# A decoder on one core: causal state products become masked score matrices, and three other stages are reordered

## The chip, the cores and the metric

The kernel runs on one core of a Trainium2 chip. A core has TensorE (matrix products, written to PSUM), VectorE, ScalarE, GpSimd and SyncE (which here only issues transfers). The metric is the device time of one execution in microseconds.

## The reference, cut to what matters

The whole kernel is a decoder of twelve layers on x of 32 x 128 x 128 (items, positions, features). The change touches the layers below. The second self attention (`_L1_attn_ref`) is a linear attention that learns at test time, with 16 heads of 8 features. Per head it takes two gradient steps and applies the states up to each position. In the form that the kernel uses, with k, q and v projected from the normalised x, W0 the first weights of a head, and tril the causal sum over positions s <= t:

```python
z1 = k @ W0
dz1 = gradient(z1, v)                         # of a layer norm of z1 against v, per head
z2 = z1 - sum_{s<=t} (k[t] . k[s]) * dz1[s]
dz2 = gradient(z2, v) + dz1
out = q @ W0 - sum_{s<=t} (q[t] . k[s]) * dz2[s]
x = x + group_norm(out) @ Wout + bout
```

The sum over s can be made in two ways: as a running state (an 8x8 matrix for each head and position, summed along the positions, then multiplied by k or q), or as a 128x128 matrix of products k[t].k[s] for each head, masked, times dz.

The other layers: `_L1_ffn_ref`, 64 experts with six chosen per token and a shared one of 176 hidden features, whose sum is added to x; `_L2_attn_ref`, a linear attention without heads, relu(q), relu(k), out = q @ (k^T v) / (q . sum k); and `_L3_xattn_ref`, a cross attention with 16 heads of 8 features on 120 context rows with softmax.

## The kernel before

x stays in SBUF for the whole kernel, `R.x`, 128 positions x 32 items x 128 features. Each layer is a phase: its own buffers and semaphores, one program for each engine, and a barrier of all engines at its end. Within a phase each engine's program is an order written out by hand. `skewed(eng, depth, n)` yields slots; in slot t, `item(lag)` stands for item t - lag, so that an engine's slot holds steps of up to depth + 1 items, each at another point of its way. The body is unrolled four times in a hardware loop, with the first and last slots outside. `written_out` does the same with no loop. `chain(...)` makes the next instruction of the same engine wait for this one. All matrix products here are f32, except biases; TensorE runs each as two instructions, each with its own load of the stationary matrix.

`l1_attn` works on pairs of items (sixteen slots with work, depth 3). ScalarE normalises, TensorE transposes and projects to five groups of 128 columns (q, k, v scaled by the norm's weights, k @ W0, q @ W0). VectorE computes `gradient` (ten operations on 256 columns), then the outer products of k and dz, 1,024 columns per item (L1203, L1214); TensorE sums them along the positions by a product with the triangular `upper` (L1260, two of 512 columns per item); VectorE multiplies the sums out of PSUM by k or q (L1158) and reduces eight columns to one (L1161). All of this is done twice per pair, for step 1 and step 2. GpSimd prepares x + bout (L1104).

`l1_slots` runs the experts on 32 pairs of experts' slots, two at a time: transfer of 128 rows and the weights, transpose (L1848), hidden products (L1855), Silu and product, output (L1863), a scatter to DRAM by GpSimd. `l1_combine` reads the six shares of each token back, reduces them on VectorE (L1908), adds the shared expert (L378, L381, L387) and makes statistics. `l2_attn` starts with a common power on GpSimd (L95) and then goes through pairs of items, two at a time.

`l3_xattn` (depth 4) per item: scores (L2921), maxima on VectorE (L2858), their transpose (L2946), scores again in the other orientation (L2950), minus the maxima by products with `pick` (L2961), exponential on ScalarE (L2909), values (L2935). The first scores of the next item use the same PSUM as the exponential, so they wait for it. Other layers that the rows show: `l_mix_p_conv` (L2393, a convolution in `l2_mix`, 128x128 stationary and 32 moving columns) and L634 (`l0_xattn`).

## Time and profile before

| | us |
|---|---|
| median of 3 runs | 4386.25 |
| lowest and highest | 4383.8, 4393.79 |
| the profiled execution, its time | 4399.44 |
| its span, from first to last instruction | 4397.5 |
| TensorE, VectorE, ScalarE, GpSimd busy | 3267.4, 2842.7, 1802.4, 681.8 |
| `l1_attn`, stretch 827 to 1364 | 537.0 |
| `l1_slots`, 1764 to 1856 | 92.0 |
| `l1_combine`, 1856 to 1953.4 | 97.4 |
| `l2_attn`, 1953.4 to 2079.4 | 126.0 |
| `l3_xattn`, 3696 to 3993 | 297.0 |

PE is TensorE, PEld its loads of stationary matrices, DVE VectorE, ACT ScalarE, POOL GpSimd, SPq SyncE's queue. Names have buffer numbers left out, so `l_attn` may be the self attention of any layer; the line tells which. PEclk, the granted clock of TensorE, is a share of 2.4 GHz: 1.00 is that, 0.50 is 1.2 GHz. A busy TensorE is not TensorE at its peak.

### The profile page before, as it was taken

The page shows a single profiled execution, that of the slowest core. Times are in us where ns is not written, and L with a number is a line of the kernel's source. Part 1 is how long each engine was busy: PE and PEld are TensorE (multiplying, and loading weights), DVE is VectorE, ACT ScalarE, POOL GpSimd, SP SyncE. Part 2 cuts the span into 40 slices and gives each one's busy share as a digit, 9 for nine tenths or more (in the row PEclk, how much of TensorE's full clock was granted, in tenths as well). Part 3 has the DMA queues.
Part 4 walks back from the last instruction along what each step waited for, and adds up shares of the span by engine and source line. Part 5 has one row for each costly group of instructions (what it writes and reads, how often), then busy time and mean ns, then how long its engine had stood idle before and what let it go on. Part 6 is the DMA issues. An engine that isn't in the chain of part 4 may idle for free. (4 is left out here: it accounts for less than half of the span.)

```text
span 4397.5 us, 70729 instructions
## 1 busy us (share of the span) xinstructions
PE 3267.4 (74%) x22305; PEld 2394.5 (54%) x22369; DVE 2842.7 (65%) x8231; ACT 1802.4 (41%) x5188; POOL 681.8 (16%) x867
## 2 busy tenths in 40 slices
PE   3668379366654886755777876999899997786887
PEld 3546269222222664534454754666577775554777
DVE  6556633499995876174898263555467775556997
ACT  1346334111112664212777233222155553435886
POOL 0045533100002777200000120000100000000000
PEclk9789589666666665577788685999999998998999
DMA  4040168200004000420300011333200000000000
GB/s 116 1 166 0 33 195 234 73 0 0 0 0 154 3 0 1 126 95 18 74 0 0 1 38 34 103 100 99 86 1 0 0 0 4 0 0 15 1 0 19
DMA packets 135723, 196.88 MB, mean 45 GB/s; under 512 B 24858, under 2 KB 90840, under 8 KB 133846
## 3 DMA queue, kind: packets, MB, share of 16 engines
q1 hardware_dynamic: 124078, 186.31, 14.0%
q0 software_dynamic: 11520, 9.05, 0.7%
q8 instruction: 60, 0.98, 0.1%
q14 instruction: 65, 0.53, 0.0%
HBM read 151.49 MB, written 58.63 MB: 48 GB/s over the span
## 5 line engine op out<-in xcount | busy, mean ns | idle before, releaser
L1260 PE MATMUL l_attn_p_s<-l_attn_outer,l_attn_upper 128*128 128x512 f32 x256 | 204.5, 973 | 113.9 <-DVE l_attn_outer L1203 100.0
L95 POOL TENSOR_TENSOR rstd<-vareps,minus_half 128x32 f32<-128x32 f32 x11 | 59.9, 5444 | 1391.7 <-DVE vareps L86 1258.0
L2583 ACT ACTIVATE l_ffn_sg<-l_ffn_p_g 128x512 f32<-128x512 f32 x168 | 100.3, 597 | 355.4 <-PE l_ffn_p_g L2620 355.4
L2554 DVE TENSOR_TENSOR l_ffn_part<-l_ffn_sg,l_ffn_share 128x512 f32<-128x512 f32 x168 | 116.3, 693 | 190.8 <-ACT l_ffn_sg L2583 183.3
L2610 PEld LDWEIGHTS l_ffn_p_o<-l_ffn_wd,l_ffn_h 128*128 128x128 f32 x1344 | 175.7, 191 | 85.2 <-issue 76.1
L1418 POOL DMA_INDIRECT slots_in<-l_xattn_x,l_xattn_slot x192 | 190.3, 991 | 83.8 <-issue 49.9
L1260 PEld LDWEIGHTS l_attn_p_s<-l_attn_outer,l_attn_upper 128*128 128x128 f32 x256 | 79.2, 324 | 218.7 <-issue 174.4
L2730 ACT ACTIVATE l_attn_E<-l_attn_p_s,l_attn_nm 128x128 f32<-128x128 f32 x512 | 181.2, 386 | 2.9 <-DVE l_attn_nm L2688 2.9
L2610 PE MATMUL l_ffn_p_o<-l_ffn_wd,l_ffn_h 128*128 128x128 f32 x1344 | 178.1, 275 | 2.3 <-DVE l_ffn_h L2557 1.6
L2620 PE MATMUL l_ffn_p_g<-l_ffn_f_xTall,l_ffn_wg 128*128 (+1 forms) x336 | 173.7, 599 | 0.5 <-DVE l_ffn_turned L2545 0.5
L2622 PE MATMUL l_ffn_p_u<-l_ffn_f_xTall,l_ffn_wu 128*128 (+1 forms) x336 | 172.5, 595 | 0.0
L2747 PEld LDWEIGHTS l_attn_p_y<-l_attn_xT,l_attn_wqkv 128*128 128x128 f32 x1024 | 130.3, 193 | 33.8 <-issue 32.4
L3141 PE MATMUL l_ffn_p_w<-ident,l_ffn_w 128*128 128x128 f32 x1024 | 127.9, 286 | 14.6 <-DVE l_ffn_w L3015 14.6
L2747 PE MATMUL l_attn_p_y<-l_attn_xT,l_attn_wqkv 128*128 128x128 f32 x1024 | 136.2, 276 | 1.6 <-DVE l_attn_qT L2692 1.5
L3141 PEld LDWEIGHTS l_ffn_p_w<-ident,l_ffn_w 128*128 128x128 f32 x1024 | 124.8, 202 | 21.3 <-DVE l_ffn_w L3015 20.4
L2557 DVE TENSOR_TENSOR l_ffn_h<-l_ffn_part,l_ffn_p_u 128x512 f32<-128x512 f32 x168 | 115.5, 687 | 5.7
L2730 ACT ACTIVATION_READ_ACCUMULATOR l_attn_E<-l_attn_p_s,l_attn_nm 128x1 f32 x512 | 115.7, 226 | 0.0
L2858 DVE TENSOR_REDUCE l_xattn_nm<-l_xattn_p_s 128x16 f32<-128x1920 f32 x32 | 69.0, 2158 | 65.6 <-PE l_xattn_p_s L2921 65.6
L2622 PEld LDWEIGHTS l_ffn_p_u<-l_ffn_f_xTall,l_ffn_wu 128*128 128x128 f32 x336 | 64.3, 191 | 81.2 <-issue 79.5
L939 DVE COPY l_experts_part<-l_experts_x 128x1 f32<-128x1 f32 x72 | 11.1, 154 | 137.9 <-DMA shares_out<-l_experts_y,l_experts_to 103.1
L2268 PE MATMUL l_film_p_m<-l_film_diag,l_film_e 128*120 128x256 f32 x256 | 93.4, 530 | 8.8 <-issue 8.6
L2909 ACT ACTIVATE l_xattn_E<-l_xattn_p_s 120x2048 f32<-120x2048 f32 x32 | 60.1, 1877 | 93.8 <-PE l_xattn_p_s L2961 93.8
(806 smaller groups left out, 9436.5 us busy)
## 6 DMA issues: line engine op xcount, KB each, us to landing
l_experts_w<-in_L_ffn_w SPq DMA_DIRECT2D x72, 512.0 KB
l_ffn_share<-share_rows SPq DMA_DIRECT2D x112, 256.0 KB, 3.2
slots_in<-l_xattn_empty SPq DMA_DIRECT2D x8, 2145.0 KB, 24.0
shares_out<-l_xattn_zero SPq DMA_DIRECT2D x24, 512.0 KB, 11.5
l_combine_got<-shares_out SPq DMA_DIRECT2D x16, 768.0 KB, 4.5
l_attn_toep<-kernel_rows SPq DMA_DIRECT2D x1, 8192.0 KB, 31.1
xattn_toep<-ssm_rows SPq DMA_DIRECT2D x1, 8192.0 KB
l_slots_w<-in_L_ffn_w SPq DMA_DIRECT2D x32, 176.0 KB
```

Source lines behind the costliest of these rows:

```text
L1260: mm = pe.matmul(p_s[:, r, a], upper[:], outer[:, r, a * 512:(a + 1) * 512], start=True, stop=True)
L1418: pool.indirect_dma_start(xb, bass.IndirectOffsetOnAxis(ap=slot[:, b, k:k + 1], axis=0), x6[:, u, k], None, bounds_check=last, oob_is_err= ...
L2268: mm = pe.matmul(p_m[0:SC, 0:256], e[:, u % 2, h], diag[:, h].rearrange("p k t -> p (k t)"), start=(h == 0), stop=(h == H - 1))
L2554: dve.tensor_tensor(part[:, w], sg[:, w], share[:, slot], ALU.mult).then_inc(s.share_used, 1)
L2557: dve.tensor_tensor(h[:, w], part[:, w], p_u[:, w], ALU.mult).then_inc(s.h_ready, 1)
L2583: act.activation(sg[:, k], p_g[:, k], ACT.Silu).then_inc(s.silu_ready, 1)
L2610: mm = pe.matmul(p_o[:, u, q * P:(q + 1) * P], h[:, (u * CH + c) % 2, q * P:(q + 1) * P], wd[:, c], start=(c == 0 and q == 0), stop=(c == ...
L2620: pe.matmul(p_g[:, k], gate_w[:, cols], x, start=True, stop=True).then_inc(s.gate_psum, 1)
L2622: pe.matmul(p_u[:, k], up_w[:, cols], x, start=True, stop=True).then_inc(s.up_psum, 1)
L2730: e = act.activation(E[:, u % 2, h], p_s[:, u % 2, odd, c * P:(c + 1) * P], ACT.Exp, bias=nm[:, u % 2, h:h + 1], accum_out=sums[:, u % 2, ...
L2747: mm = pe.matmul(p_y[:, c * P:(c + 1) * P], wqkv[:, w:w + P], xT[:, u // 2], start=True, stop=True)
L3141: mm = pe.matmul(p_w[:, c * P:(c + 1) * P], w[:, v, r, n:n + P], R.ident[:], start=(h == 0), stop=(h == H - 1))
```

## The change

*`l1_attn`*: the outer products, the sums along the positions, the multiplications and the reductions go. Keys and queries are now projected in transposed form (two products of 256 columns), and the rest as three groups of 128 columns. ScalarE copies keys and queries out of PSUM, and the keys four times more, each time with one head of every four kept (`head4`). `scored` makes sixteen products of 32 rows, 128 stationary and 128 moving columns: the 128x128 score matrices of sixteen heads of one item, in the four banks of `p_s`. VectorE multiplies them by the triangle while it takes them out of PSUM, 2,048 columns at once (`keys` for step 1, `queries` for step 2). `applied` multiplies each masked matrix (stationary, 128x128) with the eight columns of its head's dz. Per pair there are four score blocks, four masks and four product blocks. The depth is 4 instead of 3. One more transfer (`head4`) and one more small operation stand in the preparation; the bias is split for 384 columns instead of 640.

*`l1_slots`*: no loops; each slot has the transpose of item n, the hidden products of n - 1 and the output of n - 2; x and weights have four buffers instead of two.

*`l1_combine` and `l2_attn`* become one phase, `l1_out`, on pairs with depth 4. Three of the six shares are added to x by GpSimd, three by products with the identity in the PSUM group of the shared expert's output. The statistics and the power are made per pair, on two columns, and the attention of the pair follows in later slots. VectorE's slot: output of n - 4 and statistics, the expert's product of n, x and statistics of n - 1, keys and queries of n - 2, shift of n - 1. ScalarE takes over the normalisation, GpSimd the bias.

*`l3_xattn`*: the output product goes to `p_c` and, with the next item's keys, behind the second half of the shifted scores instead of ahead of it; VectorE's additions move with it.

```diff
# l1_attn, VectorE
-    def applied(psum, b, read, part, x, step):
-        for r in range(2):
-            dve.wait_ge(psum, b * 2 + (r + 1))
-            dve.tensor_tensor(square(part[:, r]), square(p_s[:, r].rearrange("p a n -> p (a n)")),
-                              over_columns(x[:, r * P:(r + 1) * P]), ALU.mult).then_inc(read, 1)
-        dve.wait_ge(read, b * 2 + 2)
-        chain(dve.tensor_reduce(step, part[:].rearrange("p r (m i) -> p (r m) i", i=HD), AX.X, ALU.add))
+    def masked(b, u, r):
+        dve.wait_ge(s.scores2_psum, b * 2 + (r + 1))
+        dve.tensor_tensor(queries[:, u % 2, r], scores, causal, ALU.mult).then_inc(s.queries_ready, 1)
-        for b, u in item(2):
-            applied(s.states2_psum, b, s.part2_read, part2, q_[u], step2[:])
-            chain(dve.tensor_tensor(qw[u], qw[u], step2[:], ALU.subtract))
+        for b, u in item(3):
+            dve.wait_ge(s.step2_psum, b * 2 + 2)
+            chain(dve.tensor_tensor(qw[u], qw[u], p_w[:, 0:W], ALU.subtract))
             dve.tensor_reduce(gs[:, 0], heads(qw[u]), AX.X, ALU.add).then_inc(s.sums_ready, 1)
-        for b, u in item(1):
-            applied(s.states1_psum, b, s.part1_read, part1, k_[u], step1[:])
-            dve.tensor_tensor(z2[:], z[u], step1[:], ALU.subtract).then_inc(s.z2_ready, 1)
-        for b, u in item(2):
+        for b, u in item(2):
+            dve.wait_ge(s.step1_psum, b * 2 + 2)
+            dve.tensor_tensor(z2[:], z[u], p_z[:, 0:W], ALU.subtract).then_inc(s.z2_ready, 1)
+        for b, u in item(1):
+            masked(b, u, 0)
...
+        for b, u in item(1):
+            masked(b, u, 1)
+        for b, u in item(1):
+            dve.wait_ge(s.std1_ready, b + 1)
+            gradient(z[u], vg[u], n1[:], d1[:], t1[:], st1)
+            dve.tensor_tensor(heads(dz1[:, u % 2]), heads(d1[:]), wide(st1[:, 1]), ALU.mult).then_inc(s.dz1_ready, 1)
...
+        for b, u in item(0):
             for r in range(2):
-                dve.tensor_tensor(square(outer2[:, r]), over_columns(k_[u][:, r * P:(r + 1) * P]),
-                                  over_rows(dz2[:, r * P:(r + 1) * P]), ALU.mult).then_inc(s.outer2_ready, 1)
...
-        for b, u in item(0):
-            dve.wait_ge(s.std1_ready, b + 1)
-            gradient(z[u], vg[u], n1[:], d1[:], t1[:], st1)
-            chain(dve.tensor_tensor(heads(dz1[:]), heads(d1[:]), wide(st1[:, 1]), ALU.mult))
-            after(dve, s.states1_psum, b * 2)
-            for r in range(2):
-                dve.tensor_tensor(square(outer1[:, r]), over_columns(k_[u][:, r * P:(r + 1) * P]),
-                                  over_rows(dz1[:, r * P:(r + 1) * P]), ALU.mult).then_inc(s.outer1_ready, 1)
+                dve.wait_ge(s.scores1_psum, b * 2 + (r + 1))
+                dve.tensor_tensor(keys[:, r], scores, causal, ALU.mult).then_inc(s.keys_ready, 1)
+            dve.wait_ge(s.sq1_ready, b + 1)
+            dve.tensor_reduce(st1[:, 0], heads(sq1[:]), AX.X, ALU.add).then_inc(s.var1_ready, 1)
...
# l1_attn, ScalarE
+            for c in range(2):
+                act.activation(kq[:, u % 2, c], p_y[:, c * W:(c + 1) * W], ACT.Identity, bias=bqk[:, c:c + 1])
+            for m in range(SUB):
+                last = act.activation(kTm[:, u % 2, :, m], side(p_y[:, 0:W]), ACT.Identity, scale=head4[:, m:m + 1], bias=bhead[:, m:m + 1])
+            last.then_inc(s.kq_ready, 1)
...
# l1_attn, TensorE
-    def states(b, r, ready, psum, outer):
-        pe.wait_ge(ready, b * 2 + (r + 1))
-        for a in range(2):
-            mm = pe.matmul(p_s[:, r, a], upper[:], outer[:, r, a * 512:(a + 1) * 512], start=True, stop=True)
-        mm.then_inc(psum, 1)
-    def projected(b, r):
-        after(pe, s.part1_read, b * 2 + (r - 1))
-        for c, cols in ((0, slice(0, 3 * P)), (1, slice(3 * P, 5 * P))):
-            wide_ = cols.stop - cols.start
-            pe.matmul(p_s[:, r, c, 0:wide_], xT[:, r * P:(r + 1) * P], wproj[:, cols], start=True, stop=False)
-            mm = pe.matmul(p_s[:, r, c, 0:wide_], ones3[:], bparts[:, cols], start=False, stop=True)
-        mm.then_inc(s.proj_psum, 1)
+    def scored(u, r, c):
+        for m in range(SUB):
+            for j in range(4):
+                rows = slice(32 * j, 32 * j + 32)
+                mm = pe.matmul(p_s[:, j, m * P:(m + 1) * P], kTm[rows, u % 2, r, m], kq[rows, u % 2, c, r * P:(r + 1) * P], start=True, stop=True)
+        return mm
+    def applied(out, a, r, dz):
+        for h in range(H):
+            mm = pe.matmul(out[:, r * P + h * HD:r * P + (h + 1) * HD], a[:, h], dz[:, r * P + h * HD:r * P + (h + 1) * HD], start=True, stop=True)
+        return mm
...
+    for item in skewed(pe, 4, PAIRS):
+        for b, u in item(3):
+            pe.wait_ge(s.sums_ready, b + 1)
+            pe.matmul(p_w[:, W:W + 2 * H], R.ones[:], gs[:, 0], start=True, stop=True).then_inc(s.mean_psum, 1)
         for b, u in item(0):
             pe.wait_ge(s.xhat_ready, b + 1)
             for r in range(2):
+                mm = pe.transpose(p_x[:, r * P:(r + 1) * P], xhat[:, r * P:(r + 1) * P], R.ident[:])
             mm.then_inc(s.xT_psum, 1)
+        for b, u in item(1):
+            pe.wait_ge(s.keys_ready, b * 2 + 2)
+            scored(u, 0, 1).then_inc(s.scores2_psum, 1)
+        for b, u in item(0):
+            pe.wait_ge(s.xT_ready, b + 1)
+            after(pe, s.proj_read, b * 2)
+            pe.matmul(p_y[:, 0:W], wproj[:, P:W], xT[:], start=True, stop=True)
+            pe.matmul(p_y[:, W:2 * W], wproj[:, 0:P], xT[:], start=True, stop=True).then_inc(s.kq_psum, 1)
+        for b, u in item(4):
             pe.wait_ge(s.ctx_ready, b + 1)
             for r in range(2):
+                mm = pe.transpose(p_x[:, W + r * P:W + (r + 1) * P], qw[u][:, r * P:(r + 1) * P], R.ident[:])
             mm.then_inc(s.ctxT_psum, 1)
+        for b, u in item(3):
+            pe.wait_ge(s.squares_ready, b + 1)
+            pe.matmul(p_w[:, W + 2 * H:W + 4 * H], R.ones[:], gs[:, 1], start=True, stop=True).then_inc(s.sqmean_psum, 1)
+        for b, u in item(1):
+            pe.wait_ge(s.queries_ready, b * 2 + 1)
+            scored(u, 1, 1).then_inc(s.scores2_psum, 1)
+        for b, u in item(4):
+            for d, _ in item(2):
+                pe.wait_ge(s.z2_ready, d + 1)
+            pe.wait_ge(s.ctxT_ready, b + 1)
             for r in range(2):
+                mm = pe.matmul(p_z[:, W + r * P:W + (r + 1) * P], cT[:, r * P:(r + 1) * P], wout[:], start=True, stop=True)
+            mm.then_inc(s.out_psum, 1)
+        for b, u in item(0):
+            pe.wait_ge(s.kq_ready, b + 1)
             for r in range(2):
+                if r == 1:
+                    pe.wait_ge(s.proj_read, b * 2 + 1)
+                pe.matmul(p_y[:, 0:3 * P], xT[:, r * P:(r + 1) * P], wproj[:, W:5 * P], start=True, stop=False)
+                pe.matmul(p_y[:, 0:3 * P], ones3[:], bparts[:], start=False, stop=True).then_inc(s.proj_psum, 1)
+        for b, u in item(1):
+            pe.wait_ge(s.dz1_ready, b + 1)
+            for c, _ in item(4):
+                pe.wait_ge(s.out_taken, c + 1)
+            for r in range(2):
+                applied(p_z, keys[:, r], r, dz1[:, u % 2]).then_inc(s.step1_psum, 1)
+        for b, u in item(0):
+            for c, _ in item(1):
+                pe.wait_ge(s.queries_ready, c * 2 + 2)
+            scored(u, 0, 0).then_inc(s.scores1_psum, 1)
+        for b, u in item(2):
+            pe.wait_ge(s.dz2_ready, b + 1)
+            applied(p_w, queries[:, u % 2, 0], 0, dz2).then_inc(s.step2_psum, 1)
+        for b, u in item(0):
+            pe.wait_ge(s.keys_ready, b * 2 + 1)
+            scored(u, 1, 0).then_inc(s.scores1_psum, 1)
+        for b, u in item(2):
+            applied(p_w, queries[:, u % 2, 1], 1, dz2).then_inc(s.step2_psum, 1)
...
# l1_slots, SyncE and TensorE
+    for n in range(NP):
+        after(sp, s.xT_psum, n + 1 - V)
+        after(sp, s.meta_ready, n + 1 - V)
+        sp.dma_start(x[:, n % V], xs[n]).then_inc(x_in[n % V], DMA)
+        after(sp, s.hid_psum, n + 1 - V)
+        sp.dma_start(w13[:, n % V], A["L1_ffn_w13"][n]).then_inc(up_in[n % V], DMA)
+        after(sp, s.y_psum, n + 1 - V)
+        sp.dma_start(w2[:, n % V], A["L1_ffn_w2"][n]).then_inc(down_in[n % V], DMA)
...
+    for item in written_out(2, NP, V):
+        for n, u in item(0):
+            pe.wait_ge(x_in[u], (n // V + 1) * DMA)
+            after(pe, s.xT_ready, n - 1)
+            pe.transpose(p_x[:, n % 2, 0:P], x[:, u, 0:D], R.ident[:]).then_inc(s.xT_psum, 1)
+        for n, u in item(1):
+            pe.wait_ge(s.xT_ready, n + 1)
+            pe.wait_ge(up_in[u], (n // V + 1) * DMA)
+            after(pe, s.h_ready, n - 1)
             for g in range(2):
                 for e in range(2):
                     w = (2 * e + g) * FP
+                    mm = pe.matmul(p_h[0:FP, n % 2, g * P + e * CAP:g * P + (e + 1) * CAP], w13[:, u, w:w + FP],
+                                   xT[:, n % 2, e * CAP:(e + 1) * CAP], start=True, stop=True)
             mm.then_inc(s.hid_psum, 1)
...
# l1_out, GpSimd
+    for item in written_out(4, PAIRS):
+        for b, u in item(2):
+            pool.wait_ge(s.xhat_ready, b + 1)
+            pool.tensor_tensor(pair(R.x, b), pair(R.x, b), both(bout), ALU.add).then_inc(s.xb_ready, 1)
+        for b, u in item(0):
+            pool.wait_ge(got_in[u], (b // V + 1) * DMA)
+            for n in range(SPLIT):
+                add = pool.tensor_tensor(pair(R.x, b), pair(R.x, b), got[:, u, :, n], ALU.add)
+                if n < SPLIT - 1:
+                    chain(add)
+            add.then_inc(s.got_added, 1)
+        for b, u in item(1):
+            pool.wait_ge(s.var_ready, b + 1)
+            pool.tensor_tensor(rs[:, u % 2], ve[:, u % 2], R.minus_half[:, 0:2], ALU.pow).then_inc(s.rstd_ready, 1)
...
# l1_out, TensorE, the second of nine steps in a slot
+        for b, u in item(1):
+            after(pe, s.x_added, b)
+            pe.wait_ge(got_in[u], (b // V + 1) * DMA)
+            for n in range(SPLIT, K):
+                pe.matmul(p_d[:, 0:W], R.ident[:], got[:, u, :, n], start=(n == SPLIT), stop=False, skip_group_check=True)
+            pe.wait_ge(s.h_ready, b + 1)
+            for r in range(2):
+                for f in range(FC):
+                    mm = pe.matmul(p_d[:, r * P:(r + 1) * P], h[:, u % 2, f, r * P:(r + 1) * P], wd[:, f * P:(f + 1) * P],
+                                   start=False, stop=(f == FC - 1), skip_group_check=True)
+            mm.then_inc(s.down_psum, 1)
...
# l3_xattn, TensorE
-        for b, u in item(4):
-            pe.matmul(p_r[:, 0], headsT[:], wo[:], start=True, stop=True).then_inc(s.out_psum, 1)
         for b, u in item(2):
             pe.wait_ge(s.shift_spread, b + 1)
-        for b, u in item(1):
-            pe.matmul(p_c[:, 0:SC], wkv[:, 0:P], cT[:, u % 2], start=True, stop=True).then_inc(s.kT_psum, 1)
-        for b, u in item(2):
             for m in range(SUB):
                 for j in range(4):
                     rows = slice(32 * j, 32 * j + 32)
                     mm = pe.matmul(p_s[0:SC, j, m * P:(m + 1) * P], pick[rows, m], nmT[rows], start=False, stop=(m == SUB - 1))
             mm.then_inc(s.shifted_psum, 1)
+        for b, u in item(4):
+            pe.matmul(p_c[:, 256:384], headsT[:], wo[:], start=True, stop=True).then_inc(s.out_psum, 1)
+        for b, u in item(1):
+            pe.matmul(p_c[:, 0:SC], wkv[:, 0:P], cT[:, u % 2], start=True, stop=True).then_inc(s.kT_psum, 1)
         for b, u in item(3):
             pe.wait_ge(s.oT_ready, b + 1)
-            after(pe, s.out_taken, b)
+            after(pe, s.heads_ready, b)
```

## Rows read from the trace of the kernel before

**Rows 1.** The page, busy time, share of the span and instructions of each engine.

```profile
PE 3267.4 (74%) x22305; PEld 2394.5 (54%) x22369; DVE 2842.7 (65%) x8231; ACT 1802.4 (41%) x5188; POOL 681.8 (16%) x867
```

**Rows 2.** Stretches: length, PE, PEld, DVE, ACT, POOL busy, clock, DMA, GB/s.

```profile
827.00:1364.00 537.00, 308.74 (x650) 137.81 (x650) 461.11 (x846) 82.42 (x225) 17.08 (x17) 0.66 0.01 2
1764.00:1856.00 92.00, 73.04 (x416) 52.85 (x416) 13.28 (x96) 29.70 (x97) 31.14 (x32) 0.50 0.46 120
1856.00:1953.40 97.40, 57.29 (x192) 33.20 (x192) 77.09 (x128) 9.69 (x17) 0.00 (x0) 0.71 0.40 132
1953.40:2079.40 126.00, 78.23 (x384) 63.16 (x384) 57.68 (x226) 25.61 (x80) 5.47 (x1) 0.78 0.01 3
3696.00:3993.00 297.00, 224.88 (x3808) 159.48 (x3808) 151.05 (x303) 110.76 (x192) 28.40 (x65) 0.95 0.01 1
```

**Rows 3.** The same view, ten slots of `l1_attn`.

```profile
934.10:1241.40 307.30, 190.84 (x400) 84.56 (x400) 281.13 (x511) 50.88 (x142) 7.25 (x10) 0.67 0.00 0
```

**Rows 4.** Groups by form in these slots: xcount, busy us, mean ns, idle before.

```profile
L1260 PE MATMUL l_attn_p_s<-l_attn_outer,l_attn_upper 128*128 128x512 f32 x160 | 130.4, 991 | 65.7 <-DVE l_attn_outer L1203 60.6 <-DVE l_attn_part L1158 5.1
...
L1158 DVE TENSOR_TENSOR l_attn_part<-l_attn_p_s,l_attn_proj 128x1024 f32<-128x1024 f32 x40 | 47.9, 1218 | 11.6 <-PE l_attn_p_s L1260 11.6
L1161 DVE TENSOR_REDUCE l_attn_step<-l_attn_part 128x256 f32<-128x2048 f32 x20 | 45.7, 2286 | 0.7
...
L1146 DVE TENSOR_TENSOR l_attn_d<-l_attn_d,l_attn_proj 128x256 f32<-128x256 f32 x20 | 8.5, 425 | 0.7
...
L1104 POOL TENSOR_TENSOR l_attn_xb<-x,l_attn_bout 128x256 f32<-128x256 f32 x10 | 7.3, 725 | 353.7 <-DVE x L1183 353.7
```

**Rows 5.** `l3_xattn`: timeline (start, length), and a stretch of its first score block.

```profile
3712.50 2.07 PE L2950 MATMUL l_xattn_p_s<-l_xattn_qT,l_xattn_kTm 32*120 32x128 f32 x32
...
3712.50:3714.50 2.00, 2.00 (x33) 1.76 (x32) 0.29 (x1) 0.00 (x0) 0.00 (x0) 0.50 0.00 0
...
3808.96 1.15 PE L2950 MATMUL l_xattn_p_s<-l_xattn_qT,l_xattn_kTm 32*120 32x128 f32 x32
...
3810.04 0.49 PE L2952 MATMUL l_xattn_p_r<-l_xattn_wo,l_xattn_headsT 128*128 128x128 f32 x2
...
3810.67 1.15 PE L2961 MATMUL l_xattn_p_s<-l_xattn_nmT,l_xattn_pick 32*120 32x128 f32 x32
...
3811.89 1.88 ACT L2909 ACTIVATE l_xattn_E<-l_xattn_p_s 120x2048 f32<-120x2048 f32 x1 [2.87 <-PE l_xattn_p_s L2961]
```

**Rows 6.** One line of `l2_mix` (ns min/median/max, first and last start), its stretch.

```profile
L2393 PE MATMUL l_mix_p_conv<-xattn_xin,xattn_toep x256: 401/401/401, 2426.6 to 2481.0; 128*128 128x32 f32 x128
...
2426.60:2481.20 54.60, 54.60 (x257) 54.60 (x257) 0.65 (x2) 5.73 (x3) 0.00 (x0) 0.50 0.00 1
```

**Rows 7.** `l2_attn`, timeline of the weight loads, and a stretch of them.

```profile
1980.93 0.30 PEld L2020 LDWEIGHTS l_attn_p_m<-ones,l_attn_k 128*128 128x128 f32 x2
1981.15 0.30 PEld L2019 LDWEIGHTS l_attn_p_m<-l_attn_k,l_attn_v 128*128 128x128 f32 x2
...
1980.90:1982.50 1.60, 1.60 (x17) 1.60 (x16) 0.86 (x3) 0.83 (x3) 0.00 (x0) 1.00 0.00 0
```

**Rows 8.** `l1_attn`, timeline, TensorE, second projection of the first pair.

```profile
854.41 1.65 PE L1267 MATMUL l_attn_p_s<-l_attn_wproj,l_attn_xT 128*128 128x384 f32 x2
...
856.41 1.22 PE L1267 MATMUL l_attn_p_s<-l_attn_wproj,l_attn_xT 128*128 128x256 f32 x2
```

**Rows 9.** `l1_slots`, timeline of two turns of its loop.

```profile
1779.87 1.06 SPq L1800 DMA_DIRECT2D l_slots_w<-in_L_ffn_w  x2
...
1781.21 2.42 PEld L1855 LDWEIGHTS l_slots_p_h<-l_slots_xT,l_slots_w 128*88 128x88 f32 x16 [0.56 <-ACT l_slots_xT L1818]
...
1785.97 2.42 PEld L1855 LDWEIGHTS l_slots_p_h<-l_slots_xT,l_slots_w 128*88 128x88 f32 x16 [0.55 <-issue]
```

**Rows 10.** A group of `l0_xattn` on GpSimd; timeline of `l1_combine`, weight loads.

```profile
L634 POOL TENSOR_TENSOR l_xattn_powers<-l_xattn_norms,minus_half 128x2 f32<-128x2 f32 x32 | 23.2, 725 | 2.7
...
1871.70 1.75 PEld L387 LDWEIGHTS l_combine_p_o<-l_combine_wd,l_combine_h 88*128 88x128 f32 x15 [0.24 <-issue]
```

More of the change, by code:

```diff
@@ L1277, in _ @@
+                pe.matmul(p_z[:, 0:P], gnb[:], wout[:], start=True, stop=True).then_inc(s.composed, 1)
                 pe.wait_ge(s.composed, 2)
-                for item in skewed(pe, 3, PAIRS):
-                    for b, u in item(2):
-                        for r in range(2):
-                            for c, _ in item(1):
-                                pe.wait_ge(s.proj_read, c * 2 + (r + 1))
-                            states(b, r, s.outer2_ready, s.states2_psum, outer2)
+                for item in skewed(pe, 4, PAIRS):
+                    for b, u in item(3):
+                        pe.wait_ge(s.sums_ready, b + 1)
+                        pe.matmul(p_w[:, W:W + 2 * H], R.ones[:], gs[:, 0], start=True, stop=True).then_inc(s.mean_psum, 1)
@@ new lines, in _ @@
+            @block.scalar
+            def _(act):
+                for item in written_out(4, PAIRS):
+                    for b, u in item(0):
+                        act.wait_ge(s.gate_psum, b + 1)
+                        after(act, s.h_ready, b)
+                        act.activation(sg[:], p_g[0:FP, :], ACT.Silu).then_inc(s.silu_ready, 1)
+                    for b, u in item(3):
+                        act.wait_ge(s.mem_psum, b + 1)
+                        mem = p_m[:, 0:2 * M].rearrange("p (r c) -> p r c", c=M)
+                        act.activation(memW[:, :, P], mem[:, :, P], ACT.Copy)
+                        act.activation(memT[:], mem[:, :, 0:P], ACT.Copy).then_inc(s.mem_ready, 1)
+                    for b, u in item(2):
+                        act.wait_ge(s.xT_psum, b + 1)
+                        act.activation(xT[:], p_t[:, 0:W], ACT.Copy).then_inc(s.xT_ready, 1)
+                    for b, u in item(3):
+                        act.wait_ge(s.memW_psum, b + 1)
+                        act.activation(memW[:, :, 0:P], side(p_m[:, 0:W]), ACT.Copy).then_inc(s.memW_ready, 1)
+                    for b, u in item(2):
+                        act.wait_ge(s.k_ready, b + 1)
+                        act.activation(v[:, u % 2], kv[:, :, P:W], ACT.Copy).then_inc(s.v_ready, 1)
+                    for b, u in item(1):
+                        act.wait_ge(s.shift_ready, b + 1)
+                        for r in range(2):
+                            last = act.activation(xhat[:, u % 2, r], row(R.x, b * 2 + r), ACT.Identity, scale=rs[:, u % 2, r:r + 1], bias=sh[:, u % 2, r:r + 1])
+                        last.then_inc(s.xhat_ready, 1)
@@ L2885, in _ @@
                                           ALU.mult).then_inc(s.heads_ready, 1)
+                    for b, u in item(4):
+                        if isinstance(b, int):
+                            dve.wait_ge(s.out_taken, b + 1)
+                        chain(dve.bn_stats(R.bn[:, u], row(R.x, b)))
+                        chain(dve.bn_aggr(R.aggr[:, u], R.bn[:, u]))
+                        if u == PER - 1:
+                            dve.tensor_copy(R.stats[:, bass.ds(b - (PER - 1), PER), :], R.aggr[:, 0:PER])
             @block.scalar
```

496 lines of the change are left out of this document (208 added, 288 removed).

## The prediction

> **What bounds the kernel now.** I began with the page: TensorE is busy 74% of the span and VectorE 65% [rows 1]. Such shares are means over many stages with different limits, so they price nothing. I then took, in the view by stretches, one stretch for each stage that the change touches [rows 2]. The second self attention takes 537 us and VectorE is busy for 461 of them; `l1_slots` takes 92 us with TensorE busy for 73; `l1_combine` (97.4 us) and `l2_attn` (126 us) follow each other with neither engine full; `l3_xattn` takes 297 us. Together they are 1,149 us of the span of 4,397.5.
>
> In `l1_attn` a slot of the pipeline (one pair of items) takes 30.7 us: ten of them fill 307.3 us [rows 3]. VectorE is busy 28.1 us of a slot, TensorE 19.1, at a mean granted clock of 0.67. VectorE bounds the stage. The rows by form [rows 4] show its large pieces: the multiplications of the states out of PSUM, 1,024 columns in 1.22 us, four to a slot, and as many outer products of the same size and time; the reductions over 2,048 columns 2.29 us, two.
>
> **`l1_attn`, VectorE.** Removed per slot: 4 x 1.22 + 4 x 1.22 + 2 x 2.29 = 14.3 us. Added: four masks of 128x2048 out of PSUM. The trace has no such multiplication; a reduction that reads 2,048 columns takes 2.29, and twice the 1,024-column multiplication out of PSUM would be 2.44. I take 2.3, so 9.2 us. VectorE keeps some 25.5 us with its gaps. If it stayed the bound, the slot would shrink by 5 us.
>
> **`l1_attn`, TensorE.** Removed: the sums along the positions, sixteen instructions of 128x512, 13 us per slot (130.4 in ten) [rows 4]. Two projections of 640 columns become 384, and two products of 256 columns are new. Added: four score blocks and four product blocks.
>
> A *score block* is sixteen products of 32 rows with 128 columns. `l3_xattn` has nearly the same block: at 3712.50 it takes 2.0 us at a granted clock of 0.50, and from 3808.96 to 3810.04, later in the stage, where its mean clock is 0.95, 1.08 us [rows 2, 5].
>
> A *product block* (`applied`) is sixteen f32 products, each with its own 128x128 stationary matrix and only 8 moving columns: what costs is loading the matrices. The nearest rows are `l_mix_p_conv`: 128 products of 128x32 with 128x128 stationary matrices, back to back from 2426.6 to 2481.2, so 54.6/128 = 0.427 us for one product [rows 6]. A block of sixteen is then 6.8 us. At the upper clock two loads follow each other in 0.22 us (1980.93 to 1981.15, around the products with `ones`, one moving column wide; granted clock 1.00) [rows 7], so a block would be 3.5 us.
>
> Which clock holds decides the whole forecast. The stretch in [rows 6] answers it as well as a trace can: TensorE was busy 54.60 of 54.60 us and the granted clock was 0.50 (1.2 GHz) throughout. It never rose, although nothing interrupted the work. The product blocks are the same kind of stream with a quarter of the moving columns, and after the change they are most of what TensorE does in this stage. I take 6.8 us. The page "TensorE: Matmul & The Clock Gate" of the Trainium skill says otherwise in its section "Why this matters for your kernels": keeping TensorE continuously busy brings the full clock. By that rule the blocks would take 3.5 us; the trace disagrees for narrow products, with 0.50 over 54.6 busy us, and the rule's result is the first rival below.
>
> TensorE per slot at the lower clock: products 4 x 6.8 = 27.3; scores 4 x 2.0 = 8.0; projections 2 x 2.0 = 4.0 (from 854.41 to 856.41, for 384 columns and the bias) [rows 8]; keys and queries 1.7 (two products of 256 columns, by columns from the same rows); transposes, two sums and the output 2.6. Sum 43.6 us, above VectorE's 25.5. TensorE becomes the bound.
>
> **The walk through a slot.** The order matters, since all four score blocks share `p_s` and `step1`, `step2` go through TensorE and back. From the end of the last product block (time 0): VectorE subtracts `step2` and sums (1.1); TensorE's mean, two transposes and the first query scores end at 4.0; the mask ends at 6.4; centring, ScalarE's square and the reduction let the mean square go at 8.1; the second query scores end at 10.6; their mask at 13.0; the gradient (ten operations of 0.42 [rows 4], 4.75) at 17.7; the output must leave `p_z` first: 18.2. Meanwhile TensorE did the projections. From there it runs alone: two product blocks 13.7, key scores 2.0, a product block 6.8, key scores 2.0, a product block 6.8: 31.3. The slot is 49.5 us. VectorE idles from about 25 to 34, queued behind `scores1_psum`: its two key masks lie under the product blocks, and its 9.2 us of masks matter only in the first part. The front part contains wide work and may get the upper clock at times, which takes 2.5 us off; I take 48.7. Sixteen slots cost 16 x (48.7 - 30.7) = +288. The incomplete slots at both ends are four and four after, three and three before, and each is longer: some 32 us beyond the sixteen against some 20 (537 less the sixteen and 26 of preparation), +12. The narrower bias preparation (384 instead of 640 columns on three rows) and an edge that gets the upper clock give back about 5. The edit costs +295. Bounds: +309 with no help of the clock, +10 if everything ran at the upper one.
>
> **`l1_slots`.** Two items take 4.76 us now (1781.21 to 1785.97) [rows 9], in which TensorE waits for the chain copy, product, Silu, product. After, each wait is for work of the previous slot. TensorE's own work per item is 1.2 us for the hidden products (16 loads in 2.42 for two items) and, at the same pace, about 0.8 for the transpose and the output: 2.0 at the clock of 0.50 that the stage has [rows 2]. SyncE issues two transfers in 1.06 us [rows 9], so three in 1.6. 32 x (2.38 - 2.0) = -12 us, and ends cost less: I take -14, bounds -5 and -27 (SyncE's limit, if the clock rose).
>
> **`l1_combine` + `l2_attn` -> `l1_out`.** The two stretches are 223.4 us from border to border [rows 2]. The largest VectorE operation, the reduction over six shares, goes away: half of it becomes three GpSimd additions per pair (0.73 each [rows 4]), the other half three products with the identity. GpSimd per pair: 0.73 + 2.2 + 0.73 for the power of two columns [rows 10] = 3.7 us. VectorE: 2.2 + 0.7 + 1.5 + 0.9 + 0.2 = 5.5. TensorE, wide work at the upper clock: gate and up 0.85, identity 1.3, down 0.9 (fifteen of the sixteen loads for two pairs took 1.75 [rows 10]), memory products 0.9, the rest 2.4: 6.3. All of it is dense and wide, as the work of `l3_xattn` late in its stage, where the clock is up [rows 5]. So 6.6 us a pair, 106 us; start, a low clock at first and four drain slots 24, borders 4: 134 us. Change 134 - 223 = -89, bounds -65 (GpSimd and VectorE hold each other up) and -100. The common power of 5.5 us and one stage border go too; they are in the 223.4.
>
> **`l3_xattn`.** Now the output product and the next keys lie between the two halves of the shifted scores: 3810.04 to 3810.67, 0.63 us [rows 5], and the loop of exponential, scores, maximum, transpose, scores, exponential is closed, so that each item pays them. After, they run under the exponential. 31 x 0.63 = -20 us; bounds -12 and -22. What covers them: the exponential's 1.88 us [rows 5], of which they and the transposes of the output take some 1.1; if it were shorter than that, the gain would go.
>
> **Sum.** +295 - 14 - 89 - 20 = +172. On the profiled execution's own time, 4399.44 (span 4397.5), that is 4571; the median of the runs shown is 13 us lower, so 4558.
>
> **Rivals.**
> *The upper clock holds in the products.* For it: the stage spends a third of its time at it even now, with TensorE busy 62% (mean clock 0.67 [rows 3]), and `l3_xattn`, which has the score blocks, 0.95 [rows 2]. Against: [rows 6]. Price: the front part of the walk, with each TensorE step at the upper clock, ends at 15.7 instead of 18.2; then two product blocks 7.0, key scores 1.1, a product block 3.5 and, since with blocks that short nothing covers the key mask, 2.3 and about 2.2 more for the last key scores, mask and block: 31.8 a slot. That is +10 for the stage (incomplete slots as above, less the preparation), net -113: 4273. It decides once a product block takes less than some 4.3 us. Faster. Chance 0.10.
> *The clock is up for part of the products*, after the score blocks. Slots near 43: +205, net +82, 4468. Chance 0.12.
> *Load and narrow product do not overlap*, so each of 64 products a slot costs 0.1 more: [rows 6] shows 0.427 with 32 columns and so speaks against. +100: 4660. Chance 0.05.
> *`l1_out` gains little*: the GpSimd additions hold up VectorE, or the clock starts low at each slot. -40 instead of -89: 4607. Chance 0.05.
> My forecast has 0.68, with its own range 4510 to 4600.
>
> **Range and chances.** From the second rival to the fourth, 4440 to 4615, leaves out the first, the third and tails. Differences under 0.2% can't be told from none here. Faster 0.09, same 0.02, slower 0.89.
>
> **What would show it.** In the profile after: `l_attn_p_z` and `l_attn_p_w` groups of 256 instructions a slot's worth near 0.21 us apart; granted clock near 0.5 to 0.6 over the stage; TensorE busy over 85% and VectorE about half; slots of 47 to 50 us between GpSimd's additions; masks 2.3 us. `l1_slots` still at 0.50 with 2.0 us an item; `l1_out` near 6.6 a pair at a clock above 0.9; `l3_xattn` period 7.9. The forecast is wrong if the product blocks take 3.5 us, and too high by 16 us for each us that the slot is shorter.

## The result and the profile after

The changed kernel takes 4587.84 us (median of 4, 4585.69 to 4590.12) against 4386.69 us: ratio 1.0456, 95% interval 1.0438 to 1.0474. It is slower by 201 us; forecast were 172, and the time of 4558 within a range of 4440 to 4615.

The view by stretches of the changed kernel: the attention, its full slots, `l1_slots`, `l1_out` (columns as in [rows 2]), and a stretch of the two product blocks of step 1. The edge at 2158.70 lies 1.3 us behind the border in the table below.

```profile
823.00:1671.50 848.50, 707.28 (x4458) 624.74 (x4458) 380.74 (x745) 112.14 (x289) 17.07 (x17) 0.53 0.01 2
...
870.00:1610.00 740.00, 647.15 (x4131) 572.99 (x4123) 349.79 (x665) 99.89 (x260) 9.43 (x13) 0.53 0.00 1
...
2074.70:2158.70 84.00, 69.88 (x416) 54.96 (x416) 13.36 (x96) 27.16 (x97) 31.03 (x32) 0.50 0.49 133
2158.70:2291.60 132.90, 119.89 (x736) 104.81 (x736) 79.74 (x304) 46.10 (x128) 57.06 (x80) 0.95 0.30 100
...
1160.10:1174.00 13.90, 13.82 (x68) 13.83 (x68) 5.96 (x19) 0.23 (x1) 0.72 (x1) 0.50 0.01 1
```

In the full slots of the attention TensorE is busy 647 of 740 us (87%; before 62% [rows 3]) at a mean clock of 0.53 (before 0.67), and VectorE 47%. I take the first transfer of each stage's SyncE queue as its border in both traces; the table adds up to the difference of the two spans.

| from border to border, us | before | after | change | forecast |
|---|---|---|---|---|
| `l1_attn` | 536.1 | 848.4 | +312.3 | +295 |
| `l1_slots` | 86.9 | 82.7 | -4.2 | -14 |
| `l1_combine` + `l2_attn` / `l1_out` | 219.8 | 134.2 | -85.6 | -89 |
| `l3_xattn` | 297.8 | 273.2 | -24.6 | -20 |
| all other stages, unchanged | 3256.9 | 3245.4 | -11.5 | 0 |
| span | 4397.5 | 4583.9 | +186.4 | +172 |

The timeline of TensorE and VectorE in one slot of the changed attention (start, duration, last column the idle time before and who ended it):

```profile
1160.18 13.79 PE L1261 MATMUL l_attn_p_z<-l_attn_dz,l_attn_keys 128*128 128x8 f32 x64 [1.08 <-DVE x L1186]
...
1173.90 2.09 PE L1256 MATMUL l_attn_p_s<-l_attn_kq,l_attn_kTm 32*128 32x128 f32 x32
...
1176.06 2.29 DVE L1202 TENSOR_TENSOR l_attn_keys<-l_attn_p_s,l_attn_upper 128x2048 f32<-128x2048 f32 x1 [9.45 <-PE l_attn_p_s L1256]
...
1184.87 7.00 PE L1261 MATMUL l_attn_p_w<-l_attn_dz,l_attn_queries 128*128 128x8 f32 x32
1185.01 2.29 DVE L1202 TENSOR_TENSOR l_attn_keys<-l_attn_p_s,l_attn_upper 128x2048 f32<-128x2048 f32 x1 [6.66 <-PE l_attn_p_s L1256]
...
1191.90 0.42 DVE L1160 TENSOR_TENSOR l_attn_proj<-l_attn_proj,l_attn_p_w 128x256 f32<-128x256 f32 x1 [3.56 <-PE l_attn_p_w L1261]
...
1196.03 2.29 DVE L1150 TENSOR_TENSOR l_attn_queries<-l_attn_p_s,l_attn_upper 128x2048 f32<-128x2048 f32 x1 [2.93 <-PE l_attn_p_s L1256]
```

Two product blocks take 13.8 us, so 6.9 a block, as forecast from [rows 6]. VectorE waits 9.45 and 6.66 us for its key masks. From the end of the last block (1191.87) the mask begins at 4.2, the forecast's 4.0. Over nine full slots GpSimd's additions lie 442.4 us apart, 49.15 us a slot.

### The profile page after: what moved, and what is told of

The parts are those of the page before. It is cut to its first block and busy times, and to the rows that moved or that the text cites. A ratio compares the mean times of both kernels' runs of the same rounds, so it can differ in the third digit from the quotient of the medians.

```text
span 4583.9 us, 78123 instructions
## 1 busy us (share of the span) xinstructions
PE 3639.4 (79%) x26336; PEld 2882.2 (63%) x26337; DVE 2704.3 (59%) x8086; ACT 1838.3 (40%) x5283; POOL 730.6 (16%) x946
## 5 line engine op out<-in xcount | busy, mean ns | idle before, releaser
L1261 PE MATMUL l_attn_p_z<-l_attn_dz,l_attn_keys 128*128 128x8 f32 x1024 | 220.8, 361 | 26.3 <-DVE x L1186 22.1
L1261 PEld LDWEIGHTS l_attn_p_z<-l_attn_dz,l_attn_keys 128*128 128x128 f32 x1024 | 219.6, 332 | 32.0 <-DVE l_attn_dz L1182 32.0
L1261 PEld LDWEIGHTS l_attn_p_w<-l_attn_dz,l_attn_queries 128*128 128x128 f32 x1024 | 220.7, 332 | 13.6 <-DVE l_attn_dz L1198 7.3
L1261 PE MATMUL l_attn_p_w<-l_attn_dz,l_attn_queries 128*128 128x8 f32 x1024 | 223.5, 362 | 7.0 <-DVE l_attn_dz L1198 7.0
L1202 DVE TENSOR_TENSOR l_attn_keys<-l_attn_p_s,l_attn_upper 128x2048 f32<-128x2048 f32 x32 | 73.3, 2291 | 261.3 <-PE l_attn_p_s L1256 261.3
L1097 POOL TENSOR_TENSOR l_attn_xb<-x,l_attn_bout 128x256 f32<-128x256 f32 x16 | 11.6, 725 | 821.6 <-DVE x L1186 807.3
L1256 PE MATMUL l_attn_p_s<-l_attn_kq,l_attn_kTm 32*128 32x128 f32 x2048 | 126.7, 417 | 5.7 <-DVE l_attn_keys L1202 4.8
L1150 DVE TENSOR_TENSOR l_attn_queries<-l_attn_p_s,l_attn_upper 128x2048 f32<-128x2048 f32 x32 | 73.3, 2291 | 81.6 <-PE l_attn_p_s L1256 81.6
```

The costliest lines, as they stand in the source:

```text
L1256: mm = pe.matmul(p_s[:, j, m * P:(m + 1) * P], kTm[rows, u % 2, r, m], kq[rows, u % 2, c, r * P:(r + 1) * P], start=True, stop=True)
L1261: mm = pe.matmul(out[:, r * P + h * HD:r * P + (h + 1) * HD], a[:, h], dz[:, r * P + h * HD:r * P + (h + 1) * HD], start=True, stop=True)
```

## The experiments

Times are medians of four or five executions. The runs with 64 columns, with half of the products, with masks made twice and with eight columns in the new order were executed once, so they have no ratio. "Slot" is the mean distance of GpSimd's additions `xb` over the twelve full slots, 49.1 us in the changed kernel and 30.7 in the kernel before.

**Three edits without the attention.** `l1_attn` is taken from the kernel before.

> The changed kernel with the second self attention of the kernel before, so three of the four edits alone. Theory (the attention alone costs, the other three gain as the stages' borders in the two traces say: -87 for the fused stage, -25 for the cross attention, -3 to -8 for the experts' slots, and nothing is passed on between stages): 4387 - 119 = 4268 us, 4262 to 4276. Rival (the edits act on each other, for example a stage starts with another clock or later transfers after a longer attention): more than 10 us away from that. Each of the three stages lasts as in the changed kernel within 1 us.

4270.34 us, ratio to before 0.9734 (0.9718 to 0.975). `l1_slots` lasts 81.9 us, `l1_out` 132.9 and `l3_xattn` 272.4, that is 0.8, 1.4 and 0.8 us less than in the changed kernel (within 1 was expected of each). The three edits gain 117 us, as expected.

**The attention alone,** in the kernel before.

> The kernel before with the changed second self attention alone. Theory (stages don't act on each other): the stage costs what it cost in the changed kernel, 848.4 against 536.1 us, so 4387 + 312 = 4699 us (4690 to 4708). Rival: a part of the 312 us belongs to what follows (transfers that start later, another clock), more than 10 us away from that.

4713.94 us, ratio 1.0748 (1.073 to 1.0766). The stage lasts 850.3 us, 2 more than in the changed kernel, so it costs the same beside other stages. The median is 6 us above the expected range: the two halves add up to +210 and together measure +201. These 9 us are not found in one stage, and stay open.

**128 moving columns per product.** Each product computes and writes more columns than it needs; the next ones write over them.

```
 for h in range(H):
-    mm = pe.matmul(out[:, r*P + h*HD : r*P + (h+1)*HD], a[:, h], dz[:, r*P + h*HD : r*P + (h+1)*HD], ...)
+    c = r * P + h * HD
+    mm = pe.matmul(out[:, c:c + WIDE], a[:, h], dz[:, c:c + WIDE], ...)      # WIDE = 128; dz padded by 128 zeros
```

> Each product of a masked matrix is given 128 moving columns instead of 8, of which the next products write over all but the first eight, so that the result is the same with the same number of loads of stationary matrices. Theory (the few moving columns are why the clock stays at 0.50): the granted clock rises above 0.9 in the product blocks, a block takes 3.6 us instead of 6.9, a slot 32 us instead of 49.0, and the time falls by 16 x 17 and some 10 at the ends, to 4300 us (4290 to 4340). Rival one (the clock stays low in this stage for another reason): clock 0.50, products of 0.43 to 0.50 us, slots of 49 to 53 us, 4585 to 4660. Rival two (the clock rises but the 128 columns cost what it gives): block near 6, slots over 44.

4370.36 us, ratio to before 0.9961 (0.9947 to 0.9975): 217 us less than the changed kernel, from sixteen times the columns, but 30 us above the expected range. First windows of 2.5 us, then the timeline of this kernel:

```profile
1155.00:1157.50 2.50, 2.50 (x16) 2.50 (x15) 2.29 (x8) 0.23 (x1) 0.00 (x0) 0.58 0.00 0
1157.50:1160.00 2.50, 2.50 (x25) 2.50 (x24) 2.36 (x7) 0.00 (x0) 0.00 (x0) 1.00 0.00 0
...
1177.50:1180.00 2.50, 0.87 (x18) 0.83 (x22) 1.39 (x5) 1.79 (x6) 0.00 (x0) 1.00 0.00 0
1180.00:1182.50 2.50, 1.32 (x27) 1.16 (x21) 1.79 (x1) 1.68 (x5) 0.00 (x0) 0.69 0.02 7
1182.50:1185.00 2.50, 2.22 (x6) 0.74 (x5) 2.36 (x6) 0.24 (x1) 0.00 (x0) 0.50 0.00 0
```
```profile
1153.87 8.91 PE L1265 MATMUL l_attn_p_z<-l_attn_dz,l_attn_keys 128*128 128x128 f32 x64 [1.83 <-DVE x L1189]
...
1163.81 3.84 PE L1265 MATMUL l_attn_p_w<-l_attn_dz,l_attn_queries 128*128 128x128 f32 x32
```

The clock column goes from 0.58 to 1.00 within the first block and a block then takes 3.84 us instead of 7.00. It falls back to 0.50 after the part of the slot in which TensorE was busy 0.87 and 1.32 of 2.5 us, waiting for VectorE. So the first pair of blocks takes 8.9 instead of 7.7, and the slot 34.8 us instead of the expected 32: the size was off, rivals one and two are out.

**64 moving columns,** the same edit with another number.

> As the one with 128 moving columns, but with 64. The experts' slots of the changed kernel stream 64 columns against stationary matrices of 128x88 and stay at 0.50 with TensorE busy 56.10 of 56.10 us, so by the theory (it is the number of columns) the clock stays at 0.50 here too: product 0.43, slot 49 us, 4580 to 4595. Rival (any number of columns beyond a few is enough): clock above 0.9 and slots of 32 us, 4300.

4598.26 us, slot 49.5, clock 0.53 over the full slots, each of the two instructions of a product 0.421 us long (0.361 with eight columns). TensorE is still at 0.50 from 1165 to 1195 us, through all four blocks of a slot. The rival is out; the time is 3 us above the expected range.

**Half of the products.** Eight products of sixteen columns in a block, so that the matrices of the odd heads are left out and the output is not the reference's.

```
-for h in range(H):                    # 8 columns
+for h in range(0, H, 2):              # 16 columns
```

> Each product block has eight products instead of sixteen, with sixteen moving columns each: the masked matrices of the odd heads are left out, and their columns are computed with those of the even heads. Theory (TensorE bounds the stage and each load of a stationary matrix costs 0.43 us): a block takes 3.45 us, a slot 4 x 3.45 = 13.8 us less, 35.2, and the time 221 us and a little for the incomplete slots less: 4350 to 4370. Rival (the closed chain through VectorE's masks and gradients bounds the slot, TensorE only fills it): less than 7 us a slot, 4475 or more.

4375.92 us, slot 35.8 (13.3 us less), stage 633.7; the time is 6 us above the expected range. Nearly all of TensorE's time for the 32 products left out comes off the slot, 13.3/32 = 0.42 us a product, so TensorE bounds it.

**Key masks twice, query masks twice,** each with a spare output first.

```
+dve.tensor_tensor(spare[:], scores, causal, ALU.mult)
 dve.tensor_tensor(keys[:, r], scores, causal, ALU.mult).then_inc(s.keys_ready, 1)      # the other run: queries
```

> The changed kernel with each key mask made twice, the first time into a spare buffer: VectorE gets 4.6 us more of masks per slot, all of it where the theory has it idle, queued behind the key scores and under the product blocks. Theory: slot unchanged, 49.0 us (within 0.3), 4588 us within 10. Rival (VectorE is in the chain there too): slot 51 to 54 us, 4625 to 4665.

> The same with the two query masks, in the front part of the slot. Theory (the front part is a chain through VectorE, one mask after the other, and nothing covers it): both extra masks are paid in full, slot 49.0 + 4.6 = 53.6 us, 16 x 4.6 = 73 us and 2 for an incomplete slot: 4655 to 4670. Rival (TensorE's own work bounds the whole slot, the front part too): slot under 50 us, under 4605.

4597.47 and 4665.1 us; slots 49.1 and 54.1, stages 857.3 and 927.8 against 848.4 us. Under the product blocks the 4.6 us of VectorE's work cost the full slots nothing; the stage's 9 us lie ahead of them, where GpSimd's first two additions are 179.6 us apart instead of 169.8. Ahead of the product blocks the same work costs 79 us, 5.0 a slot. Both times lie in their expected ranges, and the walk through the slot stands.

**The same widening elsewhere,** on top of the three edits without the attention: two convolutions (the bound of the forecast, [rows 6], is one) and the hidden products of `l1_slots`.

```
-mm = pe.matmul(p_conv[:, g % 2, j, 0:NB], toep[:, h, :], xall[:, :, h], ...)
+k = min(4, 16 - j % 16, P - h)
+mm = pe.matmul(p_conv[:, g % 2, j:j+k, 0:NB], toep[:, h, :], xall[:, :, h:h+k].rearrange("p b h -> p h b"), ...)
...
-mm = pe.matmul(p_h[0:FP, n % 2, g*P + e*CAP : g*P + (e+1)*CAP], w13[...], xT[:, n % 2, e*CAP:(e+1)*CAP], ...)
+mm = pe.matmul(p_h[0:FP, n % 2, g*P + e*CAP : g*P + e*CAP + P], w13[...], xT[:, n % 2, e*CAP:e*CAP + P], ...)
```

> The kernel with the self attention of before and the three other edits (4270 us), in which three more streams of narrow products are widened in the same way, with the same results: both convolutions, 32 moving columns to 128 (fewer at the end of a bank), and the hidden products of the experts' slots, 64 to 128. Theory (few moving columns hold TensorE at 0.50 though it is busy throughout): each convolution falls from 54.6 us to 30 (128 x 0.23, and some us until the clock is up), an item of the slots from 2.17 to 1.6 us, where SyncE's three issues bound it; 4270 - 25 - 25 - 17 = 4203 us, 4195 to 4235. Rival (the low clock of these streams has another reason): 0.50 stays, and the time is 4265 to 4290.

4255.76 us, ratio 0.9706 (0.969 to 0.9722): 15 us less than without the widening, where 67 (35 to 75) were expected. Windows of this kernel, in the first convolution and in `l1_slots`:

```profile
106.00:112.00 6.00, 6.00 (x32) 5.70 (x31) 5.24 (x4) 0.00 (x0) 0.00 (x0) 1.00 0.00 0
...
1770.00:1830.00 60.00, 53.12 (x415) 39.84 (x413) 15.02 (x94) 23.87 (x95) 30.97 (x32) 0.96 0.62 173
```

In `l1_slots` the item does as expected: clock 0.96 instead of 0.50, 1.63 us an item, 69.0 us for the stage instead of 81.9. In the convolutions the clock rises as well, but a product still takes 0.40 us (51.6 us for each convolution, 54.6 before), so next to nothing is gained. A higher granted clock alone does not make a product shorter.

**The convolution's columns in runs of four.** The 128 moving columns were 512 bytes apart; now four neighbours are read together.

```
-..., xall[:, :, h:h+k].rearrange("p b h -> p h b"), ...
+mm = pe.matmul(p_conv[:, g % 2, j:j+k, 0:NB].rearrange("p j b -> p b j"), toep[:, h, :], xall[:, :, h:h+k], ...)
```

> In the last run the clock of both convolutions rose to 1.00 but a product took 0.40 us; its 128 moving columns lie 512 bytes apart. Here the same 128 columns are read in the order that puts four neighbours (16 bytes) together, and written to PSUM at a stride instead. Theory (the stride of the moving columns costs the time): a product falls towards the 0.23 us of the attention's blocks, each convolution to 30 to 36 us, 4256 - 2 x 18 = 4220 us (4210 to 4235). Rival one (any stride, also of the result, costs it; or a read of 16 bytes is no better): 0.40 stays, 4250 to 4262. Rival two (it is slower): over 4262.

4237.62 us, ratio 0.9645 (0.9629 to 0.9662): 18 us less, where 36 were expected. One line, the convolution of `l2_mix`, in this kernel (min, median, max ns; start of the first and the last):

```profile
L2412 PE MATMUL l_mix_p_conv<-xattn_xin,xattn_toep x256: 247/277/561, 2321.4 to 2353.5; 128*128 128x128 f32 x104, 128*128 128x96 f32 x8, 128*128 128x64 f32 x8, 128*128 128x32 f32 x8
```

Both convolutions now take 32 to 33 us, 19 less (30 to 36 were expected); the time is 3 us above its expected range. Only the second one pays. After the first, TensorE waits for VectorE, as the view of waits from 108 to 140 us shows:

```profile
PE l_attn_p_t L556 <- DVE l_attn_work L100: 27.7, 1, 27.7
```

In the run before this wait was 8.9 us and ended at 137 us as well: VectorE's work sets that time, and what the first convolution gained only made the wait longer. The expectation had not looked at it.

**Another order in the attention,** with 128 columns and with eight. The first gradient moves ahead of the masks, step 1's blocks stand apart.

```
 VectorE:  subtract, sum | gradient 1 | mask | centre, squares | mask | gradient 2 | output | key masks
 TensorE:  query scores | mean, transposes, keys and queries | block 1a | query scores | block 1b | squares, output | projection, key scores | block 2a | key scores | block 2b
```

> The changed kernel with 128 moving columns, and in the attention the first gradient ahead of both query masks, so that the two product blocks of step 1 run beside the masks; the first query scores come first on TensorE, the output's addition follows the second gradient. Theory (with the clock up, the slot of 34 to 36 us is the chain masks, gradient, four blocks; now only half of the blocks stand behind a gradient): from the slot's start, gradient ends at 6.1, block 9.9, query scores 11.0, mask 13.3, second gradient 18.6, key mask and block 22.4, scores 23.5, block 27.3. Slot 27.5 us (27 to 30), stage 625 - 16 x 7.5 = 505, time 4370 - 120 = 4250 us (4240 to 4290). Rival (the clock falls again where TensorE waits for the second gradient, or another wait takes over): slot 31 to 35, 4310 to 4375.

> The same order with eight moving columns as in the changed kernel. Theory (at 0.50 TensorE's own work of 43.6 us bounds the slot, whatever the order): slot 43.6 to 45.5 us instead of 49.0, stage 848 - 16 x 4.5 = 776, time 4588 - 72 = 4516 us (4500 to 4540). Rival (the order alone, with more work in one piece, brings the clock up): under 4450.

With 128 columns 4296.68 us, ratio 0.979 (0.9774 to 0.9807), mean clock 0.93 from 870 to 1300 us, stage 550.3. The slot is 30.7 us, at the lower edge of the rival's; the time lies between the two ranges. The timeline of this kernel shows where the time is:

```profile
1145.31 0.19 DVE L1188 TENSOR_SCALAR l_attn_st<-l_attn_p_w 128x32 f32<-128x32 f32 x1 [1.59 <-PE l_attn_p_w L1307]
...
1165.51 5.46 PE L1265 MATMUL l_attn_p_z<-l_attn_dz,l_attn_keys 128*128 128x128 f32 x32 [2.30 <-DVE l_attn_dz L1171]
```

The second gradient waits 1.59 us for the sum of the squares, queued behind block 1b, and the first block of the slot takes 5.46 us instead of 3.84, after a wait.

With eight columns: 4473.98 us, stage 729.1, slot 41.7. The slot is shorter than the theory's 43.6 to 45.5 us, the time lies between the ranges of theory and rival, and the clock did not come up. TensorE is busy 612.4 of 630 us at 0.54, 40.6 us a slot. In the order as changed it was busy 43.0 of 49.1 us a slot, so 6 us were waits; why its busy time fell by 2.4 us as well was not found.

**All together.** The widened convolutions and slots, and the new order with 128 columns, the sum of the squares ahead of block 1b, the output's addition between the key masks.

> The kernel with the widened convolutions and experts' slots (4238 us, its attention of before lasts 536 us), now with the changed attention in the new order, 128 moving columns, and two more moves: the sum of the squares goes ahead of the second product block of step 1 (VectorE waited 1.6 us a slot for it, queued behind that block), and the output's addition goes between the two key masks (TensorE waited 0.4 us). Theory: slot 31.0 - 2.0 = 29.0 us, stage 550 - 32 = 518 us, time 4238 - 18 = 4220 us (4208 to 4232). Rival (the clock falls once more in the front part, or VectorE with its 23 to 25 us of work a slot holds it up elsewhere): slot 30.5 to 31, stage 540 to 550, 4238 to 4255.

4216.6 us, ratio 0.9604 (0.9591 to 0.9617), as expected. The slot is 28.2 us, 2.5 less than before the two moves (2.0 were expected of them). The stage takes 520.5 us, against 535.4 for the running states in the first experiment, and the interval lies below that of the kernel with those (0.9629 to 0.9662). The stretch of the full slots, and a block behind a wait, from this kernel's timeline:

```profile
900.00:1300.00 400.00, 354.94 (x3889) 315.60 (x3888) 319.44 (x617) 91.17 (x242) 8.71 (x12) 0.94 0.01 1
```
```profile
1149.55 3.84 PE L1268 MATMUL l_attn_p_z<-l_attn_dz,l_attn_keys 128*128 128x128 f32 x32 [2.29 <-DVE l_attn_dz L1172]
```

The block behind a wait of 2.29 us takes 3.84 us here, as the others do: the clock stood at 1.00 from 1140 to 1170 us. So with TensorE at 2.4 GHz and at work under the masks, the score matrices take 15 us less than the running states in their old order. No run gave the running states a new order of their own.

## Why the prediction was right, point by point

- **TensorE becomes the bound, at 1.2 GHz.** Right: 6.9 us a block (forecast 6.8), 2.1 for scores (2.0), masks 2.29 (2.3), slot 49.15 (48.7), clock 0.53. Shown by the half of the products (-13.3 us a slot), and by the masks made twice. What decided it was [rows 6], a stretch of the same kind of work: in the slot shown TensorE was busy without a gap from 1160.2 to 1191.8 us, and the clock stayed at 0.50. The Trainium skill, "TensorE: Matmul & The Clock Gate", section "Why this matters for your kernels", says that keeping TensorE continuously busy brings the full clock; the blocks with 8 and 64 columns disagree (0.50), those with 128 agree (1.00). Why the clock stays low in such a stream no run shows.
- **The incomplete slots** were undersized: 17 us instead of 7 (12 less 5), and the clock gave nothing back there (0.50 to 0.53 outside the full slots). With the slot's 0.4 us this makes the attention's +312 instead of +295.
- **`l1_slots`** was oversized: -4 instead of -14. An item takes 2.17 us, TensorE without a gap (busy 56.10 of 56.10 us at 0.50 from 2083.9), where I had added up 2.0; with 2.38 before that is -7 for 32 items; the other 3 us are lost at the ends, where the forecast had hoped for 2 more (the first hidden products begin 4.8 us after the first transfer, before 3.7).
- **`l1_out`** took 134.2 us where 134 were forecast, by luck. A pair takes 7.17 us instead of 6.6, TensorE busy 107.7 of 110 us at 1.00: its gate and up products take 1.73 us a pair (2200.62 to 2202.35), and 0.85 had been put in. The sixteen pairs leave 19.5 us for start, drain and borders, where 28 had been put in, and the two errors cancel. The change is -86 and not -89 since the two stages before were read as 223.4 us, and from border to border they are 219.8.
- **`l3_xattn`** -24.6 for -20: the period is 7.73 us, 0.84 less than 8.57; 0.63 was the moved work. The wait in front of the exponential fell from 2.87 us [rows 5] to 2.04, so the period lost what this wait lost; the 0.2 us beyond the moved work were not traced. Two timelines of the exponential, before (the next one begins at 3811.89 [rows 5]) and after:

```profile
3803.32 1.88 ACT L2909 ACTIVATE l_xattn_E<-l_xattn_p_s 120x2048 f32<-120x2048 f32 x1 [2.88 <-PE l_xattn_p_s L2961]
```
```profile
4013.53 1.88 ACT L2942 ACTIVATE l_xattn_E<-l_xattn_p_s 120x2048 f32<-120x2048 f32 x1 [2.04 <-PE l_xattn_p_s L2989]
...
4021.26 1.88 ACT L2942 ACTIVATE l_xattn_E<-l_xattn_p_s 120x2048 f32<-120x2048 f32 x1 [2.04 <-PE l_xattn_p_s L2989]
```

- **The 13 us between the profiled execution and the median.** Taking them off was right for the kernel before: its unchanged stages alone are 11.5 us longer in that execution than in the changed kernel's, whose profiled execution (4585.69) lies 2 us under its median. So the forecast by stages was 26 us short of the changed stages' +198 (17 + 10 + 3 - 5, rounded), and that is nearly all of 4588 - 4558.
- **The rival with the upper clock** had a wrong sum. Its slot of 31.8 us, with +12 for the incomplete slots and -5 for the preparation, gives +25 for the stage and 4288 us, not +10 and 4273; the bound of +10 has the same fault. The nearest run, with 128 columns, was dearer still: the stage takes 624.8 us, 89 more than before, and the kernel 4370. The front part is as the rival had it, 15.5 us (1172.5 to 1188.0) for 15.7. But the slot is 34.8, mainly because the four blocks take 16.6 us instead of 14.0, the first of them beginning at 0.50 after the wait, and the incomplete slots cost some 23 us where 7 were put in.

## What to carry to other kernels

Before work is moved from VectorE to TensorE, price TensorE at the clock that this kind of stream had in the trace, not at the clock of the stage that it comes into. Where a busy TensorE stands at 0.50 with loads of 128x128 matrices and few moving columns, widen the moving side with columns that the next products write over, and look at the granted clock and at the time of a block: here 64 columns gave nothing, and 128 columns at a distance of 512 bytes brought the clock but hardly any time. A wait in front of TensorE can cost twice, by itself and by the slower block behind it: 5.46 us instead of 3.84 in the first run with the new order, at 0.67 from 1165.5 to 1168 us. It need not, as the last run shows.

## What the runs showed of the hardware

- Sixteen times the moving columns made a block faster: 7.00 us with 8, 3.84 with 128. With 64, block and slot were no faster than with 8.
- At a granted clock of 1.00, 128 f32 columns took 0.24 us a product with neighbours in memory (3.84/16) and 0.40 at a distance of 512 bytes. In runs of four it was 0.23, counted over 20 us of the first convolution (174 instructions, two a product, from 85 to 105 us; 24 of its 128 products are narrower). The result was written to PSUM at a stride of 128 bytes there, and that cost nothing that shows.
- TensorE was busy without a gap for 31.6 us in the changed attention and for 56.1 us in `l1_slots`, at a granted clock of 0.50 throughout.
